# Second cross-attention of a two-layer block: keys from the stored context and one joint weight product

## The reference, cut to what matters

```python
x = x + tanh(g_xattn[0]) * attention_16_heads(layernorm(x), context)      # layer 0
x = x + tanh(g_ffn[0])   * top2_of_8_experts(layernorm(x))
q, k = layernorm(x) @ Wq + bq, context @ Wk + bk                           # layer 1
v = tanh(context @ Wv + bv)
x = x + tanh(g_xattn[1]) * softmax(q @ k.T + mask) @ v                     # one head, per sequence
x = x + tanh(g_ffn[1])   * quantised_ffn(layernorm(x))
```

## Time and profile before

| what | value |
|---|---|
| median of 3 runs | 821.13 us (815.74, 821.13, 821.61) |
| profiled execution | span 881.7 us; no time of its own outside the span is given |
| busy in the span | PE 80%, DVE 81%, ACT 64%, POOL 66% |
| TensorE clock granted, mean | 0.900 |
| DMA | 127.69 MB |

### The profile page before, as it was taken

One profiled execution on the slowest core, in us unless ns is written; L12 is line 12 of the kernel. 1 busy time (PEld: TensorE's weight loads), 2 busy tenths in 40 slices (PEclk: granted clock), 3 DMA queues, 4 the chain that ended last, 5 costly groups with the idle time before them and its releaser, 6 DMA issues. The chain is left out here.

```text
span 881.7 us, 19709 instructions
## 1 busy us (share of the span) xinstructions
PE 708.1 (80%) x6550; PEld 550.0 (62%) x6550; DVE 710.4 (81%) x1855; ACT 566.2 (64%) x1172; POOL 585.0 (66%) x570
## 2 busy tenths in 40 slices
PE   6998999999998998699369978988984789476435
PEld 3776777777776776577247767877872567233134
DVE  4999988888888998489166757767876899889988
ACT  4666566767676664576046656666766787488756
POOL 4675588888887788677746544656555898188810
PEclk9999899999999999899769989999996999755759
DMA  8414532323232222757348778878775933000005
GB/s 241 137 38 141 109 129 66 134 68 131 96 104 80 91 97 103 256 169 227 115 144 266 225 205 252 253 249 256 232 235 174 353 98 108 15 1 0 1 24 169
DMA packets 95430, 127.69 MB, mean 145 GB/s; under 512 B 20529, under 2 KB 65153, under 8 KB 94305
## 3 DMA queue, kind: packets, MB, share of 16 engines
q1 hardware_dynamic: 85760, 108.00, 40.0%
q0 software_dynamic: 8672, 17.99, 5.9%
q10 hardware_dynamic: 896, 0.43, 0.2%
HBM read 82.76 MB, written 43.53 MB: 143 GB/s over the span
## 5 line engine op out<-in xcount | busy, mean ns | idle before, releaser
L590 POOL DMA_INDIRECT m_results<-a_probs,e_to x142 | 146.9, 1035 | 106.6 <-ACT a_probs L827 59.4
L614 POOL TENSOR_TENSOR a_probs<-a_probs,a_top 128x1024 f32<-128x1024 f32 x64 | 122.0, 1906 | 57.0 <-DVE a_top L1682 56.0
L805 ACT ACTIVATE room<-a_ps_s,e_bias 128x512 f32<-128x512 f32 (+1 forms) x160 | 102.0, 652 | 85.8 <-PE a_ps_s L1111 54.8
L571 POOL DMA_INDIRECT m_tokens_to<-r_rows,r_place x128 | 133.9, 1046 | 32.3 <-issue 32.1
L1702 DVE CAST e_hp<-room 128x512 fp32r<-128x512 f32 (+1 forms) x160 | 67.8, 424 | 78.7 <-remote 32.2
L722 ACT ACTIVATE a_probs_t<-a_ps_pt 128x512 f32<-128x512 f32 x128 | 69.8, 592 | 84.5 <-PE a_ps_pt L1011 84.1
L1704 DVE TENSOR_TENSOR e_hp<-room,e_hp 128x512 fp32r<-128x512 f32 (+1 forms) x160 | 102.8, 643 | 5.5
L1634 DVE TENSOR_TENSOR a_probs<-a_ps_s,a_mask 128x1024 f32<-128x1024 f32 x64 | 77.9, 1217 | 13.4 <-PE a_ps_s L892 7.5
L995 PEld LDWEIGHTS a_ps_o<-a_vals,a_probs_t 128*64 128x64 f32 x2048 | 69.3, 140 | 30.0 <-issue 29.0
L995 PE MATMUL a_ps_o<-a_vals,a_probs_t 128*64 128x18 f32 x2048 | 77.2, 214 | 8.2 <-issue 7.0
L1682 DVE TENSOR_REDUCE a_top<-a_probs 128x16 f32<-128x1024 f32 x64 | 77.2, 1206 | 0.1
(11 more groups left out here) (422 smaller groups left out, 1901.6 us busy)
## 6 DMA issues: line engine op xcount, KB each, us to landing
e_weights<-m_weights_to SPq DMA_DIRECT2D x80, 512.0 KB
m_weights_to<-r_parts SPq DMA_DIRECT2D x8, 1024.0 KB
room<-m_tokens_to SPq DMA_DIRECT2D x31, 264.0 KB
c_two<-m_results SPq DMA_DIRECT2D x3, 1536.0 KB, 10.8
a_ctx_in<-in_ctx_dram SPq DMA_DIRECT2D x17, 256.0 KB, 2.8
m_keys_t<-n_keys SPq DMA_DIRECT2D x16, 256.0 KB
m_values<-n_values SPq DMA_DIRECT2D x16, 256.0 KB
out_dram<-x_all SPq DMA_DIRECT2D x15, 256.0 KB, 2.4
```

What stands on the lines that cost most here:

```text
L571: pool.indirect_dma_start(tokens_to, bass.IndirectOffsetOnAxis(ap=place[:, k, q:q + 1], axis=0), rows[:, c % RING, q % CT, k, :], None).th ...
L590: pool.indirect_dma_start(results, bass.IndirectOffsetOnAxis(ap=to[:, v, r:r + 1], axis=0), y[:, v, r], None).then_inc(returned[v], 16)
L614: pool.tensor_tensor(probs[:, j], probs[:, j], top[:, j].unsqueeze(2).broadcast_to([P, HEADS, SEQ]), ALU.subtract).then_inc(shifted, 1)
L805: act.activation(h[:, c, at], ps_h[c][:, at], ACT.Gelu_apprx_tanh, bias=bias[:, n % ROWS, c:c + 1]).then_inc(h_sb, 1)
```

## The change

- **First attention.** PE's and ACT's `next_keys` go, with their waits. `store_keys` becomes `store_context`, which writes `ctx_t` itself at the head of SP's turn; as `ctx_t` is one buffer, `copy_context(n)` waits for the store of context n-1. The buffer `keys1` goes, and two first uses of the experts' buffer `hp` wait for other rows sent.
- **Experts.** `wq1` and `bq1` are loaded after the W1 and W2 loads of expert tile 19. Ahead of the last expert tiles PE transposes both weights, DVE adds a shift to the transposed query weights (so that a normalised row plus one gives the query bias) and PE multiplies: `Wk @ wq_t` and its product with the key bias; DVE copies both out. `constants` has one more memset.
- **Second attention.** `keys_of(n)` takes the place of `queries(n)`: the joint weights times the *stored context*, evicted with the joint bias; the normalised, transposed x (plus one, added in the eviction) goes straight into the scores. Both have two buffers. The wait for the load of n moves from `scores(n)` to `keys_of(n)`. SP loads context n after `keys_of(n-4)`.
- The last stage is as before.

```diff
@@ first attention, SP
-        def store_keys(v):
+        def store_context(v):
             at = ST * ((v + 1) % SUPERS)
-            sp.wait_ge(k1_sb, v + 1)
-            sp.dma_start(g["keys_t"][:, at:at + ST], keys1[:, v % 2]).then_inc(keys_out[v % 2], 16)
+            sp.wait_ge(ct_sb, v + 2)
+            sp.dma_start(g["context_t"][:, at:at + ST], ctx_t[:]).then_inc(context_out, 16)
@@ SP, loop over s: store_context(s - 1) behind load_ctx, store_keys(s - 1) gone
@@ SP, experts, n == EARLY + 6
+                sp.dma_start(g["wq1"][:], d["L1_xattn_Wq"]).then_inc(q1_in, 16)
+                sp.dma_start(g["bq1"][:], d["L1_xattn_bq"].rearrange("(p a) -> p a", a=1)).then_inc(q1_in, 16)
@@ POOL, constants
-            pool.memset(eps[:], LN_EPS).then_inc(terms, 1)
+            pool.memset(eps[:, 0:1], LN_EPS).then_inc(terms, 1)
+            pool.memset(eps[:, 1:2], 1.0).then_inc(terms, 1)
@@ ACT
         def copy_context(n):
             act.wait_ge(ct_ps, n + 1)
+            if n >= 2:
+                act.wait_ge(context_out, 16 * (n - 1))
-                    next_keys(s)
@@ PE
-                    next_keys(s)
-        pe.wait_ge(k1_sb, SUPERS)
+            if t == ETILES - 1:
+                pe.wait_ge(q1_in, 32)
+                pe.transpose(ps_1[:, 0], g["wq1"][:], ident[:])
+                pe.transpose(ps_1[:, 1], wk1[:], ident[:]).then_inc(both_pe, 1)
@@ PE, behind the last part
+        pe.wait_ge(both_dve, 5)
+        pe.matmul(ps_1[:, 2], wk1[:], wq_t[:], start=True, stop=True)
+        pe.matmul(ps_1[:, 3, 0:1], wq_t[:], bk1[:], start=True, stop=True).then_inc(both_pe, 1)
@@ DVE, split(0, c)
-                dve.wait_ge(sent[0], rows_sent(NCH - RING))
+                dve.wait_ge(sent[c // 2], rows_sent(NCH - RING + c // 2))
@@ DVE, ahead of L1801
+            dve.wait_ge(both_pe, 1)
+            dve.tensor_reduce(shift[:], ps_1[:, 0], AX_X, ALU.add).then_inc(both_dve, 1)
+            dve.tensor_copy(wk1[:], ps_1[:, 1]).then_inc(both_dve, 1)
+            dve.wait_ge(both_dve, 1)
+            dve.tensor_tensor(shift[:], g["bq1"][:], shift[:], ALU.subtract).then_inc(both_dve, 1)
+            dve.wait_ge(both_dve, 3)
+            dve.tensor_scalar(shift[:], shift[:], 1.0 / DM, None, ALU.mult).then_inc(both_dve, 1)
+            dve.wait_ge(both_dve, 4)
+            dve.tensor_scalar(wq_t[:], ps_1[:, 0], shift[:, 0:1], None, ALU.add).then_inc(both_dve, 1)
@@ DVE, behind first_sums(0)
+            dve.wait_ge(both_pe, 2)
+            dve.tensor_copy(g["wq1"][:], ps_1[:, 2]).then_inc(both_dve, 1)
+            dve.tensor_copy(g["bq1"][:], ps_1[:, 3, 0:1]).then_inc(both_dve, 1)
@@ second attention, SP
         for n in range(DEEP, SUPERS):
+            sp.wait_ge(k_ps, n - DEEP + 1)
+            load_context(n)
             sp.wait_ge(s_ps, n - DEEP + 1)
-            load_keys(n)
             load_mask(n)
@@ ACT (evict_x: Identity with bias eps[:, 1:2], two buffers)
-        def evict_q(n):
-            act.wait_ge(q_ps, n + 1)
-            if n >= 1:
-                act.wait_ge(s_ps, n)
+        def evict_keys(n):
+            act.wait_ge(k_ps, n + 1)
+            if n >= 2:
+                act.wait_ge(s_ps, n - 1)
@@ PE
-        def queries(n):
-            pe.wait_ge(xt_sb, n + 1)
-            if n >= 1:
-                pe.wait_ge(q_sb, n)
-            pe.matmul(ps_q[:]..., wq[:], xn_t[:], start=True, stop=True).then_inc(q_ps, 1)
+        def keys_of(n):
+            if n:
+                pe.wait_ge(k_in[n % DEEP], nth_load(n))
+                pe.wait_ge(k_sb, n)
+            pe.matmul(ps_k[:]..., w_both[:], context[n % DEEP][:], start=True, stop=True).then_inc(k_ps, 1)
@@ scores(n)
-            pe.wait_ge(q_sb, n + 1)
-            if n:
-                pe.wait_ge(k_in[n % DEEP], nth_load(n))
+            pe.wait_ge(k_sb, n + 1)
+            pe.wait_ge(xt_sb, n + 1)
```

More of the change, by code:

```diff
@@ L99, in layer0_and_experts @@
         parts = first("r_parts", [P, 2, 4, HID], F32R)
-        keys1 = first("n_keys1", [P, 2, ST], F32)
         values1 = first("n_values1", [P, 2, QUAD, DM], F32)
@@ L193, in layer0_and_experts @@
     loaded = [sem(f"a_loaded{b}") for b in range(CTX_RING)]
-    keys_out, values_out = ([sem(f"n_{n}_out{u}") for u in range(2)] for n in ("keys", "values"))
+    values_out = [sem(f"n_values_out{u}") for u in range(2)]
     (gates_in, q_in, k_in, v_in, mask_in, wo_in, ident_step, gates_ready, bq_set, scale_set, stats1, step1, var_ready,
@@ L209, in layer0_and_experts @@
          "padded"))
-    (kv_in, k1_ps, k1_sb, v1_ps, v1_raw, v1_sb) = (sem("n_" + n) for n in (
-        "kv_in", "k1_ps", "k1_sb", "v1_ps", "v1_raw", "v1_sb"))
+    (kv_in, context_out, v1_ps, v1_raw, v1_sb, q1_in, both_pe, both_dve) = (sem("n_" + n) for n in (
+        "kv_in", "context_out", "v1_ps", "v1_raw", "v1_sb", "q1_in", "both_pe", "both_dve"))
     names = ("xt_ps", "xt_hi", "xt_lo", "h_ps", "h_sb", "h_hi", "h_lo", "h_used", "yt_sb", "yr_ps", "to_ready", "y_out")
@@ L333, in _ @@
             load_ctx(s + CTX_RING)
+            if s:
+                store_context(s - 1)
             e = (s - 3) // 2
@@ L924, in values @@
             mm.then_inc(v_ps, 1)
-        def next_keys(v):
-            if v + 1 < SUPERS:
-                pe.wait_ge(k_sb, v * 4 + 8)
-            else:
-                pe.wait_ge(ct_sb, SUPERS + 1)
-            if v == 0:
-                pe.wait_ge(kv_in, 64)
-            pe.matmul(flat(ps_1), wk1[:], ctx_t[:], start=True, stop=True).then_inc(k1_ps, 1)
         def next_values(v):
@@ L1807, in _ @@
         first_sums(0)
+        weights_of_both()
         dve.wait_ge(w_pe, 1)
@@ L1893, in layer1_attention @@
     warm = sb("c_warm", [P, 1], F32)
-    wq, bq = g["wq1"], g["bq1"]
-    keys_t = [g["keys0"]] + [sb(f"c_keys{n}", [P, ST], F32) for n in range(1, DEEP)]
+    w_both, b_both = g["wq1"], g["bq1"]
+    context = [g["keys0"]] + [sb(f"c_context{n}", [P, ST], F32) for n in range(1, DEEP)]
     vals = [g["values0"][:].rearrange("p (k c) -> p k c", c=DM)] + [sb(f"c_vals{n}", [P, QUAD, DM], F32) for n in range(1, DEEP)]
@@ L1912, in bank @@
         return ctx.enter_context(nc.psum_tensor(name, [P, QUAD, P], F32))
-    ps_x, ps_q, ps_pt = (bank(f"c_ps_{n}") for n in ("x", "q", "pt"))
+    ps_x, ps_k, ps_pt = (bank(f"c_ps_{n}") for n in ("x", "k", "pt"))
     ps_s, ps_o = ([bank(f"c_ps_{n}{u}") for u in range(2)] for n in "so")
@@ L1956, in load_results, with load_context @@
             load_two(sp, g, n, later_two[:, first - IN_ROOM:end - IN_ROOM])
-        def load_keys(n):
-            sp.dma_start(keys_t[n % DEEP][:], g["keys_t"][:, n * ST:n * ST + ST]).then_inc(k_in[n % DEEP], 16)
+        def load_context(n):
+            sp.dma_start(context[n % DEEP][:], g["context_t"][:, n * ST:n * ST + ST]).then_inc(k_in[n % DEEP], 16)
         def load_mask(n):
@@ L2081, in _ @@
         evict_x(0)
-        act.wait_ge(ahead_in, 96)
-        evict_q(0)
+        act.wait_ge(ahead_in, 64)
+        evict_keys(0)
         roots(1)
@@ L2118, in transpose_x @@
             mm.then_inc(xt_ps, 1)
-        def queries(n):
-            pe.wait_ge(xt_sb, n + 1)
-            if n >= 1:
-                pe.wait_ge(q_sb, n)
-            pe.matmul(ps_q[:].rearrange("p a b -> p (a b)"), wq[:], xn_t[:], start=True, stop=True).then_inc(q_ps, 1)
+        def keys_of(n):
+            if n:
+                pe.wait_ge(k_in[n % DEEP], nth_load(n))
+                pe.wait_ge(k_sb, n)
+            pe.matmul(ps_k[:].rearrange("p a b -> p (a b)"), w_both[:], context[n % DEEP][:], start=True, stop=True)\
+                .then_inc(k_ps, 1)
         def scores(n):
             u = n % 2
-            pe.wait_ge(q_sb, n + 1)
-            if n:
-                pe.wait_ge(k_in[n % DEEP], nth_load(n))
+            pe.wait_ge(k_sb, n + 1)
+            pe.wait_ge(xt_sb, n + 1)
             if n >= 2:
@@ L2138, in scores @@
                 tok = slice(P * k, P * k + P)
-                mm = pe.matmul(ps_s[u][:, k], q[:, tok], keys_t[n % DEEP][:, tok], start=False, stop=(k == QUAD - 1))
+                mm = pe.matmul(ps_s[u][:, k], xn_t[:, u, tok], keys[:, u, tok], start=False, stop=(k == QUAD - 1))
             mm.then_inc(s_ps, 1)
         transpose_x(0)
-        pe.wait_ge(ahead_in, 96)
-        queries(0)
+        pe.wait_ge(ahead_in, 64)
+        keys_of(0)
         transpose_x(1)
@@ L2156, in _ @@
             if s + 1 < SUPERS:
-                queries(s + 1)
+                keys_of(s + 1)
             if s >= 1:
@@ L2640, in flamingo @@
             "magic": whole.enter_context(nc.sbuf_tensor("magic", [P, 2], F32)),
-            "eps": whole.enter_context(nc.sbuf_tensor("eps", [P, 1], F32)),
+            "eps": whole.enter_context(nc.sbuf_tensor("eps", [P, 2], F32)),
             "wq1": whole.enter_context(nc.sbuf_tensor("wq1", [P, DM], F32)),
```

65 lines of the change are left out of this document (30 added, 35 removed).

## The result

| | before | after |
|---|---|---|
| median, 20 runs each | 818.91 us (814.56 to 822.54) | 824.64 us (818.76 to 830.42) |
| ratio | | 1.0074, 95% interval 1.0052 to 1.0097 |
| span of the profiled execution | 881.7 us; a second one 817.3 us | 823.0 us; a second one 824.1 us |
| PE busy in the two profiles | 708.1 and 684.5 us | 686.6 and 684.8 us |

The change makes the kernel slower, by 0.74%: less than the 1% that I had called the limit of a measurement, but the interval excludes a ratio of 1. Against the second profile of before, PE is even busy 0.3 to 2.1 us longer, although 16 products that held it for about 0.9 us each are gone: what is left runs more slowly.

The account below looks back on a forecast made before the run. No single engine was taken as the bound: PE looked full in even first-attention steps, DVE in odd steps and the second attention. Terms -2.3 + 0 + 0 + 1.3 = -1.0 us, scaled to -0.9, gave 820.2 us; range 809.5 to 829.5.

Parts of the forecast that it names:

- Sum: -2.3 us: First attention: the removed product mostly fills a hole before L1020, so dropping it gains only 2.3 us; bounds 0.5 and 14.2.
- rival B: First attention: idle left by the removed product drops PE to half clock; +11.0 us, 832.1 us; chance 0.12.
- +1.3 us: Second attention: the moved load wait at n = 4 delays DVE 2.0 us, less 0.7 paid back; bounds -1 and +6.
- Only n = 4 showed a DMA as releaser: Second attention: argument against more frequent stalls, since only that load was seen releasing the scores in the stretch.
- rival C: Second attention: the moved wait stalls more often, +6 us in place of +1.3, giving 824.6 us; chance 0.08.
- So nothing of that reaches the end: Second attention's start: the first product's saved 0.78 us wait is hidden by DVE's 5.28 us DMA wait; priced at nothing.
- ACT's eviction at 0: First attention: removing ACT's eviction gains 0, as it lay between others with 4 us of ACT idle per step.
- The new wait on the store at 0: First attention: copy_context(n) waiting for the previous context's store costs 0, the store being issued about one step ahead.
- Start of the experts at 0: First uses of hp wait for later rows with 13 us of slack: 0; the added memset at most +0.15 us.
- end of the experts at 0: Two more loads and small DVE and PE operations hide in existing waits: 0, bounds 0 and +1 us.
- The ratio 0.931: Whole kernel: timed runs taken as shorter than the profiled span by this factor, turning -1.0 us into -0.9 us.
- Rival A: First attention: PE sets the pace in even steps, so removing the product gains fully; -12.0 us, 809.1 us; chance 0.25.

Follow-up runs that it names:

- 9: Kernel before with the first attention's key product cut from 512 columns to one, everything else kept: ratio 0.9999 to the kernel before.
- 6: Changed kernel with context 1 loaded into its own buffer at the end of the experts, outside the crowded queues: ratio 1.0009 to the kernel before.
- 13: Changed kernel with an ACT operation of 128x512 back at the old eviction's place, PE's product still out: ratio 1.0048 to the kernel before.
- 8: Changed kernel with the removed 128x512 product back on PE at j = 2, its result overwritten: ratio 1.0006 to the kernel before.
- 10: Changed kernel with half the removed product (128x256) back on PE at j = 2: ratio 0.9980 to the kernel before.
- 11: Changed kernel with three of the removed products on PE at j = 2: ratio 1.0065 to the kernel before.
- 3: Changed kernel with the whole second attention of before, query product included: ratio 1.0018 to the kernel before.
- 7: Changed kernel with 12 filler products on PE ahead of its wait for the load of context 1: ratio 1.0036 to the kernel before.
- 4: Changed kernel with the load of context 1 issued ahead of the experts' results load: ratio 1.0024 to the kernel before.

## Why the prediction was wrong

It forecast no change, -0.1%, and the kernel is 0.4 to 0.7% slower. By its own steps:

- **"Sum: -2.3 us" for the first attention** is the first step that failed. The mechanism behind it held: L1020 (now L1004) waits for L1617 (now L1605) in all 16 tiles, PE shows a hole of 0.73 us, and nothing gets faster (9: 0.9999 with the product's work gone). What failed is that the hole was priced at nothing. Seven profiles of the change without its product have first attentions of 314.2 to 317.5 us (mean 316.5), five with a whole or half product 310.9 to 315.1 us (mean 313.1). So the term is about +3 us in the changed kernel, not -2.3. The likely cause, argued from the rows and not proved (see below), is rival B, "The clock falls into the hole", at about a quarter of its price: not eight more falls but about two that count. My argument against B, that the fall in rows 5 followed 1.69 us of idle, took one fall for the rule; the fall shown above came behind two waits of 0.92 and 0.73 us, with PE busy 1.08 of 2 us. But one row doesn't make the rule either: behind the same two waits the clock stayed at 1.00 in the first profile. The sentence of the Trainium skill that activity releases the throttle ("TensorE: Matmul & The Clock Gate", Part 1) agrees with the row of the fall, 1.08 of 2 us busy and then 0.50, but doesn't by itself tell the two profiles apart; I had it the right way round in the rival and not in the sum.
- **The second attention, "+1.3 us".** The mechanism (the moved wait, ACT's exponentials behind the key eviction, DVE waiting for them) is what happened, at another load first. "Only n = 4 showed a DMA as releaser" was read as "only the load of 4 is tight". That row says which load was late for the scores; the wait moved to a place that PE reaches earlier. For step 1 the product stood at 682.94 and the scores at 684.74 in the timeline of before, and the load landed between them, 6.5 us after its issue at 677.28. The sum left that out, and also that the first product would no longer wait for x. The wait is 2.8 and 3.4 us, the step-4 wait 0.67 and 2.17 us, and 0 to 2 costs +1.9 to +3.4 us. At step 4 the predicted chain shows in full only where step 1 doesn't wait (6: 4.13 us in PE, 1.62 in DVE against the 2.0 forecast). It is nearest to rival C, whose 824.6 is by chance the measured median: its +6 had been put at steps 4 to 6, none of the loads for 5 and 6 made a product wait, and the first attention's +3 wasn't in it.
- **"So nothing of that reaches the end"** (the first product doesn't wait for x): it does reach it, as a loss. PE comes earlier to a load that isn't there and idles, in one of two profiles straight into the half clock.
- **ACT's eviction at 0:** right (13). **The new wait on the store at 0:** right, no copy waited for it.
- **Start of the experts at 0, end of the experts at 0:** right; 26.8 and 27.3 us against 27.4, and 22.6 and 22.7 against 22.7. The 0.92 us at L1809 that was to hide DVE's new operations is missing in the second profile of before as well, so it isn't what made them free.
- **The ratio 0.931:** wrong in kind, small in effect.
- **"32 records of a mean 0.592 us":** 0.592 is the smallest in the earlier trace rows, 0.595 the median; no term hangs on it.
- **Rival A** (PE sets the pace): excluded by 8 and 9.

**What stays open.** Cutting the product alone out of the kernel before lost as much clock and no time (9), while in the changed kernel putting it back gave 0.37%. Nor does the lost work tell the kernels with a product from those without: 6.7 to 17.6 us against 10.2 to 19.4. Where the falls land seems to decide, and the profiles don't show why they land in both the third and the ninth step in four of the seven kernels without it. Also open: the load of context 1 lands 7.9 us after its issue in both profiles of the changed kernel and in 13, all without the product, and 6.5 us in the three with one and the same order of loads (8, 10, 11). It isn't the product that makes the difference, since 3 and 7, without one, have 6.2 and 6.3 us; what does is not shown. The difference carries part of what the product seems to be worth: those three take 10.9 to 11.4 us for 0 to 2 against 12.2 to 13.8. So 0.37% for the product is an upper value for what it does in the first attention.

## What to carry to other kernels

A wait that moves to an earlier place must be checked against every load that it waits for, at the time at which the engine will reach the new place, not only against the one that was late at the old one. Where a queue is full, a load can't be put first without making another late; a slot outside the crowd is worth looking for. Work that fills a hole between two engines had no cost here (9: 0.9999 without it), and taking it out could cost: price the idle that you create, and try filler before believing in it. Profile the same kernel twice before pricing terms from one trace.

## What the runs showed of the hardware

- The granted clock fell after short waits, not only after long ones: PE busy 1.08 of 2 us, then 0.65 and 0.50. It doesn't always: after the same waits, 1.09 of 2 us busy, it stayed at 1.00 in another execution of the same kernel. With three products in the hole it didn't fall once in the first attention (0.0 us lost) against 6.7 to 19.4 us in the others.
- Work lost at half clock and time are different things: 19.2 us lost with a first attention of 313.8 us (9), 10.2 us lost with 314.2 us (4), 15.8 us lost with 317.3 us (13).
- A 256 KB load issued right behind a 1 MB one landed 6.2 to 7.9 us after its issue, in kernels with the same order of loads there.
- A single profiled execution carried 55 us of stalls (18.39 us at one instruction) that a second one of the same program didn't show.
